# Two fused weight matrices loaded from the other queue, their products split around the first turning, and VectorE's early work in a new order

## The reference

```python
h = relu(layernorm(x))
# layer 1: graph attention and a gated graph convolution on h
hh = h @ W_sa
e = where(adj != 0, exp(-leaky_relu(s_left[:, None] + s_right[None, :])), 0)   # s = hh @ a_sa halves
x_a = (e / (e.sum(1) + 1e-5)) @ hh
x_b = adj @ (h @ W_gcnb) + b_gcnb
attn_a, attn_b = sigmoid([adj @ h, h] @ Wa.T + ba), sigmoid([adj @ h, h] @ Wb.T + bb)
x = x + sigmoid(attn_a * x_a + attn_b * x_b)
# layer 2: attention inside each of 32 graphs of 64 nodes
h = relu(layernorm(x))
q, k, v = h @ Wq.T + bq, h @ Wk.T + bk, h @ Wv.T + bv
a = where(mask, q @ k.T / 16, 0)                       # mask: same graph
scores = (a + adj + adj) * where(mask, 1, -1e6)
x = x + (softmax(scores) * mask) @ v
```

## Time and profile before

| | |
|---|---|
| time, median of 3 runs | 232.29 us (231.71 to 234.67) |
| profiled execution, from its first to its last instruction | 231.0 us |
| TensorE busy | 222.2 us (96%) |
| VectorE busy | 183.1 us (79%) |
| ScalarE busy | 160.1 us (69%) |
| GpSimd busy | 61.9 us (27%) |
| mean granted clock of TensorE, share of 2.4 GHz | 0.993 |

### The profile page before, as it was taken

One profiled execution on the slowest core, in us unless ns is written; L12 is line 12 of the kernel. 1 busy time (PEld: TensorE's weight loads), 2 busy tenths in 40 slices (PEclk: granted clock), 3 DMA queues, 4 the chain that ended last, 5 costly groups with the idle time before them and its releaser, 6 DMA issues. The chain is left out here.

```text
span 231.0 us, 5379 instructions
## 1 busy us (share of the span) xinstructions
PE 222.2 (96%) x2042; PEld 194.5 (84%) x2042; DVE 183.1 (79%) x452; ACT 160.1 (69%) x308; POOL 61.9 (27%) x115
## 2 busy tenths in 40 slices
PE   7899999999999999999999999999999999999971
PEld 6788888888888888888888888888888889999951
DVE  2589778899995967599984499987699949997783
ACT  3768835899966764995651794666995855888760
POOL 4525860000034000001910001730012043576540
PEclk9799999999999999999999999999999999999999
DMA  6999399007989100752400000000000000012123
GB/s 186 359 374 386 113 332 387 15 0 248 285 316 386 44 3 0 259 177 111 173 12 4 0 0 4 1 3 0 3 0 0 3 0 4 0 50 79 48 72 128
DMA packets 20092, 26.34 MB, mean 114 GB/s; under 512 B 1889, under 2 KB 11873, under 8 KB 20065
## 3 DMA queue, kind: packets, MB, share of 16 engines
q1 hardware_dynamic: 19376, 25.71, 32.2%
q10 hardware_dynamic: 688, 0.27, 0.4%
HBM read 23.88 MB, written 2.10 MB: 112 GB/s over the span
## 5 line engine op out<-in xcount | busy, mean ns | idle before, releaser
L1091 PE MATMUL bank_a<-hd,e_hi 128*128 128x257 f16 x256 | 70.3, 274 | 0.0
L1089 PE MATMUL bank_a<-hd,e_hi 128*128 128x257 f16 x256 | 69.7, 272 | 0.0
L1093 PE MATMUL bank_a<-hd,e_lo 128*128 128x257 f16 x256 | 69.4, 271 | 0.0
L1065 PE MATMUL bank_b<-hb,adjt 128*128 128x259 f16 (+1 forms) x512 | 66.5, 273 | 0.2 <-DVE xb L1661 0.2
L1065 PEld LDWEIGHTS bank_b<-hb,adjt 128*128 128x128 bf16 x512 | 49.3, 97 | 7.5 <-DVE xb L1661 0.5
L704 ACT ACTIVATE e_hi<-e_slot 128x1024 f16<-128x1024 f32 x32 | 33.6, 1051 | 26.7 <-PE bank_a L1093 15.6
L1669 DVE SCALAR_TENSOR_TENSOR e_slot<-e_slot,adjt 128x1024 f32<-128x1024 f32 x32 | 39.0, 1219 | 9.0 <-ACT e_slot L697 9.0
L1675 DVE SCALAR_TENSOR_TENSOR e_lo<-e_slot,e_hi 128x1024 f16<-128x1024 f32 x32 | 39.0, 1219 | 7.3 <-ACT e_hi L704 7.2
L697 ACT ACTIVATE e_slot<-s_row,nbias 128x512 f32<-128x512 f32 x64 | 42.3, 709 | 0.2
L570 POOL TENSOR_TENSOR rs_all<-veb,half_neg 128x2 f32<-128x2 f32 x8 | 6.6, 823 | 88.2 <-DVE veb L1848 88.2
L1089 PEld LDWEIGHTS bank_a<-hd,e_hi 128*128 128x128 f16 x256 | 24.7, 96 | 4.0
(11 more groups left out here) (238 smaller groups left out, 380.8 us busy)
## 6 DMA issues: line engine op xcount, KB each, us to landing
adjt<-in_adj_t SPq DMA_DIRECT2D x16, 1024.0 KB, 9.1
x_all<-in_x SPq DMA_DIRECT2D x4, 512.0 KB, 5.3
out<-adjt SPq DMA_DIRECT2D x16, 128.0 KB, 1.9
adjt<-in_x SPq DMA_DIRECT2D x3, 512.0 KB, 7.4
diag<-in_adj SPq DMA_DIRECT2D x16, 64.0 KB, 3.6
adjt<-in_x SPq DMA_DIRECT2D x2, 256.0 KB, 3.7
e_slot<-in_L_gnn_W_gcnb ACTq DMA_DIRECT2D x1, 256.0 KB, 4.0
e_slot<-in_W_saT SPq DMA_DIRECT2D x1, 256.0 KB, 4.8
```

The costliest lines, as they stand in the source:

```text
L1065: eng.matmul(B[:, r % 2, 0:cols], adjt_block(k, j, r), hb16[:, j, part, 0:cols], start=(j == 0 and part == 0), stop=(j == NT - 1 and part ...
L1089: eng.matmul(A[:, r, 0:D + 1], high, hd16[:, j, 0, 0:D + 1], start=(j == 0), stop=False, skip_group_check=True)
L1091: eng.matmul(A[:, r, 0:D + 1], high, hd16[:, j, 1, 0:D + 1], start=False, stop=False, skip_group_check=True)
L1093: mm = eng.matmul(A[:, r, 0:D + 1], low, hd16[:, j, 0, 0:D + 1], start=False, stop=(j == NT - 1), skip_group_check=True)
```

## The change

- SyncE's queue: W_saT moves ahead of a_lr and the second piece of x; Wq and Wk leave it.
- ScalarE's queue: W_gcnb, then Wq, Wk, then gate_w (which now signals `w4_loaded`), then the bias columns. ScalarE's square of W_gcnb waits for W_gcnb alone. TensorE's product with W_saT and VectorE's square of the gate columns wait for all three loads of `w4_loaded`.
- TensorE: `query_key` takes its half `c` as argument; half 0 stands ahead of `turn_h(0)`, half 1 behind it; `query_bias` moves behind `times_weights(0)`.
- VectorE: the weight's low half and columns come ahead of `moments(2)`, `variance(2)` and `shift(2)`; `hT_low(1)` ahead of `shift(2)` and `moments(3)`; `hb_low(0)` ahead of `shift(3)` and `moments(4)`.

```diff
             load_batch(0)
+            eng.dma_start(w_saT, W_saT.rearrange("(k p) d -> p k d", p=P)).then_inc(w4_loaded, 16)
             eng.dma_start(a_lr[:, :, :], a_col).then_inc(w4_loaded, 16)
             load_batch(1)
-            eng.dma_start(w_saT, W_saT.rearrange("(k p) d -> p k d", p=P)).then_inc(w4_loaded, 16)
-            eng.dma_start(wq, Wq.rearrange("(k p) d -> p k d", p=P)).then_inc(qk_loaded, 16)
-            eng.dma_start(wk, Wk.rearrange("(k p) d -> p k d", p=P)).then_inc(qk_loaded, 16)
             load_batch(2)
...
             eng.dma_start(w_b[:, :, 0:D], W_gcnb.rearrange("(k p) d -> p k d", p=P)).then_inc(wb_loaded, 16)
-            eng.dma_start(w_b[:, :, D:D + 4], gate_w).then_inc(wb_loaded, 16)
+            eng.dma_start(wq, Wq.rearrange("(k p) d -> p k d", p=P)).then_inc(qk_loaded, 16)
+            eng.dma_start(wk, Wk.rearrange("(k p) d -> p k d", p=P)).then_inc(qk_loaded, 16)
+            eng.dma_start(w_b[:, :, D:D + 4], gate_w).then_inc(w4_loaded, 16)
             eng.dma_start(bqk_col[:, :, :], bq_bk).then_inc(bqk_loaded, 16)
...
-            eng.wait_ge(wb_loaded, 16 * 2)
+            eng.wait_ge(wb_loaded, 16)
             eng.activation(junk_a[:, 0, :, :], w_b[:, :, 0:D], ACT.Square, accum_out=sq[:, 0:1]).then_inc(sq_made, 1)
...
-            def query_key():
+            def query_key(c):
...
-                for c in range(KT):
-                    for kk in range(KT):
-                        eng.matmul(B[:, c, 0:D + 1], wq[:, kk, c * P:(c + 1) * P], wk_b[:, kk, :],
-                                   start=(kk == 0), stop=(kk == KT - 1))
+                for kk in range(KT):
+                    eng.matmul(B[:, c, 0:D + 1], wq[:, kk, c * P:(c + 1) * P], wk_b[:, kk, :],
+                               start=(kk == 0), stop=(kk == KT - 1))
...
-            eng.wait_ge(w4_loaded, 16 * 2)
+            eng.wait_ge(w4_loaded, 16 * 3)
...
+            query_key(0)
             turn_h(0)
-            query_key()
+            query_key(1)
             turn_h(1)
-            query_bias()
...
             times_weights(0)
+            query_bias()
             turn_h(2)
...
             shift(0)
-            eng.wait_ge(wb_loaded, 16 * 2)
+            eng.wait_ge(w4_loaded, 16 * 3)
             eng.tensor_tensor(cols_sq[:, :, 0:4], w_cols[:, :, 0:4], w_cols[:, :, 0:4], ALU.mult).then_inc(w4_squared, 1)
...
-            moments(2)
             eng.wait_ge(wb_hi_made, 1)
             eng.wait_ge(mul_made, 1)
             eng.scalar_tensor_tensor(out=wb16[:, :, 1, 0:D], in0=w_b[:, :, 0:D], scalar=w_mul[:, 0:1],
...
-            variance(2)
             eng.wait_ge(mul_made, 2)
...
-            shift(2)
             eng.wait_ge(wb_col_made, 1)
             eng.tensor_tensor(wb16[:, :, 1, D:WB], w_cols, wb16[:, :, 0, D:WB], ALU.subtract) \
                .then_inc(wb_col_made, 1)
+            moments(2)
+            variance(2)
+            hT_low(1)
+            shift(2)
             moments(3)
-            hT_low(1)
             variance(3)
+            hb_low(0)
+            shift(3)
             moments(4)
-            shift(3)
-            hb_low(0)
             variance(4)
```

## The result

The changed kernel takes 237.4 us (median of 4 runs, 236.94 to 237.69), the kernel before, beside it, 233.09 (231.71 to 234.67): ratio 1.0188, 95% interval 1.0123 to 1.0252. The profiled execution spans 235.7 us instead of 231.0.

The account below looks back on a forecast made before the run. TensorE, busy 222.2 of 231.0 us, was taken to bound the kernel through its stream's start, clock and holes. Transfers 2.0, split 0.5 and VectorE's order 1.0 added +3.5 to 232.3, giving 235.8 us, range 231.9 to 238.0.

Parts of the forecast that it names:

- Transfers: DMA queues in the head: both share one total, so gate_w lands at 8.6 us, x tiles 2, 3 at 7.9.
- What the late loads do: Head of VectorE, TensorE and ScalarE: late gate_w and x delay norms, gate products and h; 2.0 us.
- Fused products split: TensorE's head: the second half covers too little, so turning 1 waits about 0.95 us; 0.5 net of warm passes.
- VectorE's order: VectorE's head: moments of pair 2 and later shifts come late, delaying turnings 2 and 3; 1.0 us.
- The sum: Whole kernel: 2.0 from transfers, 0.5 from the split, 1.0 from VectorE's order; +3.5 us on 232.3 gives 235.8.
- 1.3 us lie around the span: Whole kernel before: median 232.29 against profiled span 231.0 us; differences were summed on the profile and added to the median.
- main case: Whole kernel: late loads, split and VectorE's order cost +3.5 us, 235.8, own range 234.2 to 236.6; chance 0.58.
- the clock stays at 1.2 GHz beyond 12.6 us: Rival, TensorE's head: work up to 16 us doubles, partly in holes; +1.5 us more, 237.3; chance 0.15.
- Loads cost nothing: Rival, head: gate_w lands before 7 us, x before 6.5, only the new orders cost; 233.3 us; chance 0.15.
- Faster: Rival, head: W_saT lands sooner and VectorE's delays hide behind TensorE's backlog; -0.4 us, 231.9; chance 0.12.

Follow-up runs that it names:

- run with the small loads first: Changed kernel with gate_w and the bias columns ahead of Wq and Wk on ScalarE's queue; 237.41 us, ratio 1.0122 to the kernel before.
- split-only run: Kernel before with the fused products split around the first turning and query_bias behind the first weights product, old loads and VectorE order; 233.85 us, ratio 1.0050.
- loads-only run: Kernel before with the changed kernel's loads and semaphores, TensorE and VectorE orders as before; 235.7 us, ratio 1.0103.
- last run: Kernel before with 3 and 3 extra products of constants and VectorE's weight low half ahead of moments of pair 2; 233.14 us, ratio 0.9942.
- the third part's end and the fourth: Runs with extra products of constants to hold TensorE's clock, the final two on the kernel before with VectorE's low half moved; those two took 232.5 and 233.14 us.
- loads-only run with extra products: Kernel before with the new loads, old orders, and 8 and 1 products of constants in TensorE's waits; 233.53 us, ratio 1.0032.

## Why the prediction was right, step by step

I predicted 235.8, +3.5 us; it came to 237.4, +4.3, the direction, the order of the stages and most landings as written.

- **Transfers: right.** gate_w was predicted at 8.6, the bias columns at 9.0, x at 7.9, W_gcnb at 5.2; TensorE had the first at 8.39, the others came at 8.86, 8.04 and 4.86. The equal share of large packets held on the whole. Two details were off and cancelled: small packets cost more than I gave them. a_lr held SyncE's queue for most of 5 to 6 us where I had 0.3 us, so Wk had left by about 6.4 us and not 7.1; and gate_w's own took 1.0 us (6.4 to 7.4) where I had half a microsecond.
- **What the late loads do: right.** The start of TensorE's own stream, 10.62 for 11.05, is near. The run with the small loads first shows that the two late loads bind together, as the step said of VectorE's queue. 2.0 us were predicted, and 1.85 measured with the clock held.
- **Fused products split: the hole was predicted where it was not.** 0.95 us ahead of turning 1, minus what warm passes give back, assumed 2.4 GHz from 12.6 us. The clock was at 1.2, the second half took 1.92 us and filled the hole. With the clock held the hole is there, 0.79 us. And the moved bias products, booked as cover, cost by themselves, by ScalarE's copy (the split-only run).
- **VectorE's order: right in kind, too small.** 1.0 us predicted; alone it cost 1.4 us by the ratio, 1.0 by the spans and 1.6 within the stream; both waits stood where predicted.
- **The sum: partly luck.** Four terms were off. The kernel before, 232.29 in its first three executions, took 233.09 beside the changed one: half of the 1.6 us by which 235.8 missed is this base. The reading that 1.3 us lie around the span was a sign of it: where an execution has both on record, they are 1.7 to 1.9 us apart, so the profiled one belongs with some 232.8. The rest is the difference, 3.5 for 4.3. The two orders were given 1.5 us together and cost 2.0 with the clock held; the lower clock, given nothing in the main case, adds some 0.5; the loads were 0.15 too dear.
- **The clock.** I gave the rival "the clock stays at 1.2 GHz beyond 12.6 us" 0.15 and 1.5 us, 237.3. It is what happened in the profiled execution. Its price was smaller: the first weights product came 0.7 us after the predicted 15.35, the product of pair 2 0.6 after 22.4. That its 237.3 is the measured 237.4 is chance, for it stands on the low base. My argument against it, that half of the fused products and the turning stand there, was no evidence. TensorE was also idle for 1.98 us just before, where the kernel before had waited 0.35.
- **The rivals.** "Loads cost nothing" gave 233.3, the loads alone cost 2.4 us: excluded. "Faster" needed gate_w by 6.7: it came at 8.39. The Trainium skill's rule (DMA: Bandwidth & Descriptors, "Issuing engines are not separate DMA queues") agrees with the packets and with the loads-only run: the second queue brought no more bytes per microsecond (354 GB/s in 5 to 6 us and 330 in 6 to 7, before 339 and 351), and put two small loads behind two large ones.

## What to carry to other kernels

Moving a large load to another queue moves what stands behind it there: order all queues together by when each load is first waited for, small ones included. Making a result sooner pays only if someone waits for it; look for the waiter in the trace before reordering, since what is pushed back may have one. While TensorE waits at the head for a transfer, cheap products in the wait can pay: here they took 1.9 us off the changed kernel. And before a part of a loss is put down to the clock, hold the clock in both kernels: at the mark it took 2.15 us off the changed kernel and 1.7 off the kernel before.

## What the runs showed of the hardware

**The recorded clock can be wrong before its first change.** In the profile of the split-only kernel the granted clock reads 1.00 throughout the head, yet until about 14 us its products run at half speed: four passes of the fused products took 2.06 us, as in the changed kernel where 0.50 is recorded, and the gate products 1.71 us instead of 1.05. The profile of the last run (3 and 3 products) shows the same. The split-only kernel's windows and timeline, then the gate products of the last run:

```profile
11.00:12.00 1.00, 1.00 (x5) 0.71 (x4) 0.98 (x5) 0.00 (x0) 0.28 (x2) 1.00 1.06 389
```
```profile
7.02 1.71 PE L1259 MATMUL bank_b<-a_lr,e_slot 128*128 128x2 f32 x8
...
9.82 2.06 PE L1106 MATMUL bank_b<-wk_b,wqk_in 128*128 128x257 f32 x4
```
```profile
7.99 1.71 PE L1260 MATMUL bank_b<-a_lr,e_slot 128*128 128x2 f32 x8
```

In these two profiles a product's own length tells the clock, and the record does not.

**The head's clock spreads the times of one program.** 35 executions of the kernel before, made beside the runs of the third part's end and the fourth, took 231.25 to 235.31 us and lie in groups: four at 231.2 to 231.7 with a mean recorded clock of 0.997 or 0.998, sixteen at 232.3 to 233.4 (14 of them 0.991 to 0.993), fourteen at 234.1 to 234.6, of which thirteen record 1.00; one took 235.31. That the thirteen ran low from the start with nothing recorded is inferred from the last paragraph; none of them was traced. The last run's profile, recorded as 0.998, is of that kind. The three kernels with old loads and extra products, all but equal, had one execution of each kind profiled: mark at 33.10, 34.58 and 36.82, time 231.23, 232.69 and 235.00 us. Why one execution falls into one group and not another was not tested. It means that a median of three can be off by a microsecond here: the kernel before read 232.29 in its first three runs and 233.1 to 233.6 later. Holding the clock in the changed kernel narrowed ten runs to 1.0 us.

**The clock can fall at the end as well.** From the mark to TensorE's last group of products it is 191.1 us in twelve of the fourteen profiles. In the loads-only run it is 191.7, with a granted clock of 0.50 from 228 us on, and in the loads-only run with extra products 191.9, with 0.50 from 226 us on: 0.6 and some 0.85 us of their spans that have nothing to do with the change in the head.
